# A decoder layer on one core: the key projection at the end of a step, and five other pieces at other places

## The chip, the cores and the metric

One core of a Trainium2 chip runs the whole kernel. The metric is the device time of one execution in microseconds (us), median of several runs. Engines: PE is TensorE (matmuls), DVE is VectorE, ACT is ScalarE, POOL is GpSimd, SP only issues DMAs here.

## The reference

A post-norm decoder layer for 32 sequences x of 256 tokens with 256 features, all in float32.

```python
x1 = layernorm(x + self_attention(x))      # 16 heads of 16, q and k widened to rank 32, causal softmax
x2 = layernorm(x1 + cross_attention(x1))   # 120 context rows; scores over all 256 features; mask after softmax
x3 = layernorm(x2 + ffn(x2))
# ffn: xr = mu_r*x + (1-mu_r)*x_prev, xk = mu_k*x + (1-mu_k)*x_prev   (x_prev: the token before)
#      out = sigmoid(xr @ W_r.T) * (relu(xk @ W_k.T)**2 @ W_v.T)
```

## The kernel before

One "batch" is one sequence. Work is pipelined over steps: `step(at)` handles five batches at once, each at another stage, `Batch(at, skew)` being batch `at - skew`. The stages are IN (skew 0: q and k), SCORES (2: self-attention scores and their row maxima, and v), PROBS (3: the turned scores, exp, product with V, and kx and vx for the cross-attention), CROSS (4: output projection z1, x1, cross-attention s2, g, z2) and FFN (5: x2 turned, k3, r3, v3). Steps 5 to 31 have all stages live; 0 to 4 fill the pipeline, 32 to 36 empty it.

Each engine runs its own list of operations, written out by hand in its `step`, and waits on semaphores for the others. Within a list nothing overtakes.

PE goes through six slots in the order 0, 2, 3, 1, 4, 5. In `slot(c)` it computes scores of one group of heads into `ps_s` (8 heads in slots 0 and 1, 4 in the others) and turned scores of another batch into `ps_t`. Slot after slot uses the same `ps_s` and `ps_t`, so each needs the row maximum of the slot before (DVE, L918, `max_done`) and its exp (ACT, L718, `exp_done`). Between the slots stand the projections and the rest: q (L492), z1 (L500), x2's turning (L463), k (L492), x1's turning (L463), v (L500), s2 (L649), k3 (L492), r3 (L500), g (L666), PV(0) (L594), v3 (L500), z2 (L680), PV(1) (L594), kx (L472), vx (L480). A projection in split precision is 12 matmuls: weights and data are each a high and a low part, three products are summed. For it an ACT operation writes the high part and a POOL or DVE operation the low part: xT, yT, xk, xr, k_act. q and k are split after their projection, into `parts0` and `parts1` (ACT L727, DVE L926).

All the pieces between the slots share two PSUM banks, `ps_m0` and `ps_m1`. `BANK_USERS` lists the users of each in order, with the semaphore that says a user's result has been read; `bank_free` makes PE wait for that of the user before.

DVE, in order: the maximum of slot 0; x3's statistics; the maximum of slot 2; q's low part; sum1 (L988); x1's statistics (L935, L941); the maximum of slot 3; k's low part; the mix for xk; the maximum of slot 1; the mix for xr; the maximum of slot 4; s2's maximum (L1005); s2's reciprocal (L1010) and a_nrm; the maximum of slot 5; the shift (L1021 to L1029); k_act's low part (L975); the first half of the attention output; the gated product; sum2 and x2's statistics; the second half.

The mix, on DVE, reads `dx` and `x2T` in SBUF:

```python
last = nc.vector.scalar_tensor_tensor(dst[:, k, :], dx[:, k, :], cols[:, mu, k:k + 1],
                                      x2T[:, k, 0:T], op0=ALU.mult, op1=ALU.add)
```

POOL, in order: yT's low part; x_res plus a constant; 1/deviation and offset of x3 and of x1 (L1126 to L1132); dx; xk's low part (L1156); xr's low part (L1159); x1p; xT's low part of the next batch; sum3; offset of x2.

SP issues the DMAs in order: x_in for the next batch; q's parts to DRAM; the outputs; k's parts; x_res; ctxT; the shift of this step to DRAM and back into two rows of the stack (L378, L384); and then the stack, twelve DMAs of 128 KB each (L347), which regroup q's and k's parts by head. The scores read the stack two steps after the projections, the turned scores also the shift.

Of the kernel before, what the change touches and what calls it, by code (L numbers as in the profile page):

```python
# [14 lines left out]
RING = 3  # L15
# [31 lines left out]
def decoder_layer(nc, x, x_turned, ctx_turned, mask_in, Wq, bq, WkT, bk, WvT, bv, WoT, bo, Wq_lsr_turned, Wk_lsr_turned,  # L47
# [8 lines left out]
    with es:  # L56
# [116 lines left out]
        def sems(*names):  # L173
# [9 lines left out]
        a_ = sems("xT_hi", "q_hi", "k_hi", "v_ready", "yT_hi", "x1T_ready", "a_exp_done", "g_ready",  # L183
# [12 lines left out]
                  "gated_done", "xr_ready", "xk_ready", "k_act_lo")  # L196
# [106 lines left out]
        def _(sp):  # L303
# [45 lines left out]

            def step(at):  # L350
                b = Batch(at, IN)
                if live(at + 1, IN):
                    sp.wait_ge(g_["xT_lo"], b.n + 1)
                    sp.dma_start(x_in[:], tokens(x_turned, b.n + 1).rearrange("(k p) t -> p k t", p=P)).then_inc(x_loaded, 16)
                if live(at, IN):
                    save_parts(b, 0, "q_lo")
                if live(at - 1, FFN):
# [4 lines left out]
                if live(at, IN):  # L362
                    save_parts(b, 1, "k_lo")
# [4 lines left out]
                if live(at, SCORES):  # L368
# [4 lines left out]

                    if c.n >= RING:
# [26 lines left out]
        def _(pe):  # L401
# [135 lines left out]
            def step(at):  # L537
# [84 lines left out]
                filler(4, not on[FFN] and not on[IN])  # L622
# [604 lines left out]
```

## Time and profile before

| | |
|---|---|
| median of 3 runs | 970.09 us (968.84 to 973.53) |
| the profiled execution | 973.32 us |
| its span in the profile | 971.6 us |
| PE busy | 918.1 us (94%) |
| DVE, ACT, POOL busy | 715.0, 590.1, 450.6 us |
| mean granted TensorE clock | 0.971 of full speed |

The span goes from the first instruction to the last. Busy time is that in which the engine works at something; PE's is modelled at the ends of matmuls, so it reads a little high. A duration in a timeline is that of a single operation or of several merged (x2, x8); the next operation of an engine may start before the last one's end, so what an operation costs its engine is read from start to start.

### The profile page before, as it was taken

The page shows a single profiled execution, that of the slowest core. Times are in us where ns is not written, and L with a number is a line of the kernel's source. Part 1 is how long each engine was busy: PE and PEld are TensorE (multiplying, and loading weights), DVE is VectorE, ACT ScalarE, POOL GpSimd, SP SyncE. Part 2 cuts the span into 40 slices and gives each one's busy share as a digit, 9 for nine tenths or more (in the row PEclk, how much of TensorE's full clock was granted, in tenths as well). Part 3 has the DMA queues.
Part 4 walks back from the last instruction along what each step waited for, and adds up shares of the span by engine and source line. Part 5 has one row for each costly group of instructions (what it writes and reads, how often), then busy time and mean ns, then how long its engine had stood idle before and what let it go on. Part 6 is the DMA issues. An engine that isn't in the chain of part 4 may idle for free.

```text
span 971.6 us, 25805 instructions
## 1 busy us (share of the span) xinstructions
PE 918.1 (94%) x9597; PEld 723.6 (74%) x9597; DVE 715.0 (74%) x1565; ACT 590.1 (61%) x1153; POOL 450.6 (46%) x667
## 2 busy tenths in 40 slices
PE   6789999999999999999999999999999999999975
PEld 5456778778777777777778777777778777777653
DVE  3646778788788878788778877878878887867442
ACT  2125566666776666666776666666776666656643
POOL 6202354544455455544445445454445545434453
PEclk9959999999999999999999999999999999989998
DMA  8977876656677766666688877666678777611000
GB/s 221 195 146 117 149 131 111 137 129 137 129 147 150 151 117 106 136 136 133 132 143 149 150 122 123 119 133 134 129 144 148 150 134 116 110 30 31 24 12 22
DMA packets 121447, 119.73 MB, mean 123 GB/s; under 512 B 28201, under 2 KB 104811, under 8 KB 121195
## 3 DMA queue, kind: packets, MB, share of 16 engines
q1 hardware_dynamic: 121323, 118.08, 64.3%
q8 instruction: 77, 1.26, 0.6%
q14 instruction: 47, 0.39, 0.2%
HBM read 75.05 MB, written 42.99 MB: 121 GB/s over the span
## 4 chain that ended last, share of the span: by engine, by line
PE 80%; ACT 8%; issue 5%; DVE 4%; POOL 2%; DMA 1%; SPq 0%; ACTq 0%; POOLq 0%; DVEq 0%
PE ps_m L500 20%; PE ps_m L492 11%; PE ps_o L594 9%; PE ps_s L513 8%; PE ps_t L513 5%; PE ps_s L528 4%; PE ps_m L463 4%; PE ps_m L649 3%; PE ps_m L472 3%; ACT p L718 3%; ACT sum L735 3%; PE ps_m L680 3%; PE ps_m L666 3%; PE ps_m L480 3%; PE ps_t L528 2%
## 5 line engine op out<-in xcount | busy, mean ns | idle before, releaser
L918 DVE TENSOR_REDUCE row_max<-ps_s 128x4 f32<-128x1024 f32 (+1 forms) x192 | 233.2, 1215 | 76.7 <-PE ps_s L528 76.5
L718 ACT ACTIVATE p<-ps_t 128x1024 f32<-128x1024 f32 x192 | 196.4, 1023 | 45.2 <-PE ps_t L528 45.1
L513 PE MATMUL ps_s<-stack 48*128 48x128 f32 (+1 forms) x1024 | 109.1, 313 | 15.5 <-DVE row_max L918 6.4
L827 ACT COPY kxT<-ps_m 128x240 f32<-128x240 f32 x32 | 11.5, 358 | 169.0 <-PE ps_m L472 169.0
L513 PEld LDWEIGHTS ps_s<-stack 48*128 48x128 f32 x1024 | 73.3, 190 | 53.4 <-DVE row_max L918 20.0
L1100 POOL TENSOR_TENSOR xT_lo<-x_in,xT_hi 128x512 fp32r<-128x512 f32 x32 | 41.4, 1293 | 151.4 <-ACT xT_hi L705 151.4
L594 PE MATMUL ps_o<-p,v_pad 128*32 128x256 f32 (+1 forms) x2048 | 96.3, 329 | 0.0
L513 PE MATMUL ps_t<-stack 50*128 50x128 f32 (+1 forms) x1024 | 93.1, 281 | 1.9 <-ACT p L718 1.4
L594 PEld LDWEIGHTS ps_o<-p,v_pad 128*32 128x32 f32 x2048 | 57.4, 109 | 43.2 <-issue 21.2
L1171 POOL TENSOR_TENSOR sum<-r_tanh,x 128x512 f32<-128x512 f32 x32 | 40.9, 1279 | 83.4 <-DVE r_tanh L1039 83.4
L513 PEld LDWEIGHTS ps_t<-stack 50*128 50x128 f32 x1024 | 75.3, 192 | 5.0 <-ACT p L718 2.7
L935 DVE BATCH_NORM_STATS2 bn<-sum 128x6 f32<-128x256 f32 x192 | 71.9, 417 | 3.6 <-POOL sum L1171 1.4
L1156 POOL TENSOR_TENSOR xk_lo<-r_tanh,xk_hi 128x512 fp32r<-128x512 f32 x32 | 41.3, 1290 | 66.5 <-ACT xk_hi L772 66.5
L1126 POOL TENSOR_TENSOR var<-mv,eps 128x2 f32<-128x2 f32 x96 | 18.8, 196 | 114.2 <-DVE mv L941 110.7
L1129 POOL TENSOR_TENSOR rstd<-var,neg_half 128x2 f32<-128x2 f32 x96 | 66.9, 697 | 0.0
L528 PE MATMUL ps_s<-mask_s,identb 64*64 64x256 bf16 (+1 forms) x768 | 66.1, 334 | 0.0
L528 PE MATMUL ps_t<-mask_t,identb 64*64 64x256 bf16 (+1 forms) x768 | 61.8, 312 | 0.0
L1159 POOL TENSOR_TENSOR xr_lo<-dx,xr_hi 128x512 fp32r<-128x512 f32 x32 | 41.3, 1290 | 40.9 <-ACT xr_hi L788 40.9
L1140 POOL TENSOR_TENSOR yT_lo<-y32T,yT_hi 128x512 fp32r<-128x512 f32 x32 | 40.6, 1270 | 40.9 <-ACT yT_hi L743 40.9
L952 DVE STREAM_TRANSPOSE yu<-ps_o 128x512 f32<-128x512 f32 x64 | 44.8, 701 | 16.6 <-PE ps_o L594 16.6
L968 DVE SCALAR_TENSOR_TENSOR dx<-dx,cols,x2T 128x256 f32<-128x256 f32 x64 | 54.0, 882 | 0.0
L926 DVE SCALAR_TENSOR_TENSOR parts<-ps_m,cols,parts 128x256 fp32r<-128x256 f32 x64 | 28.0, 480 | 29.8 <-ACT parts L727 29.8
(167 smaller groups left out, 2715.0 us busy)
## 6 DMA issues: line engine op xcount, KB each, us to landing
stack<-parts_dram SPq DMA_DIRECT2D x384, 128.0 KB, 5.8
parts_dram<-parts SPq DMA_DIRECT2D x64, 512.0 KB, 4.8
x_in<-in_x_turned SPq DMA_DIRECT2D x32, 256.0 KB, 8.2
x_res<-in_x SPq DMA_DIRECT2D x32, 256.0 KB, 4.0
out_x<-sum SPq DMA_DIRECT2D x64, 128.0 KB, 4.7
ctxT<-in_ctx_turned SPq DMA_DIRECT2D x32, 120.0 KB, 3.7
shift_dram<-shift_turned SPq DMA_DIRECT2D x64, 16.0 KB
stack<-shift_dram SPq DMA_DIRECT2D x64, 16.0 KB
```

Of the source, the lines that this page charges most:

```text
L492: last = nc.tensor.matmul(bank[:, a * T:(a + 1) * T], ww, ss, start=(e == 0), stop=(e == len(terms) - 1))
L500: last = nc.tensor.matmul(bank[:, j * C:(j + 1) * C], ss, ww, start=(e == 0), stop=(e == len(terms) - 1))
L513: nc.tensor.matmul(target[:, at_h:at_h + width], left[b.slot][r0:r0 + rows_n, h // 2, rows_at:rows_at + P], right[b.slot][r0:r0 + rows_n, ...
L528: last = nc.tensor.matmul(o, identb[r, 64 * half:64 * half + 64], mask[r, block, 0:o.shape[1], :], start=False, stop=True, skip_group_chec ...
L594: last = nc.tensor.matmul(ps_o[VW * j:VW * (j + 1), half, at_g + T - width:at_g + T], v_pad[b.slot][:, tile, h, :], p[c][:, at_h:at_h + wi ...
L718: nc.scalar.activation(p[c][:], ps_t[:], ACT.Exp).then_inc(exp_done[c], 1)
L918: nc.vector.tensor_reduce(row_max[:, :, j0:j0 + nj, tile], ps_s[:].rearrange("p (g j w) -> p g j w", j=nj, g=2), AX_X, ALU.max) \
L935: last = nc.vector.bn_stats(bn[i][:, j, :], src[:, j, :])
L952: nc.vector.transpose(turned, ps_o[:, half, :]).then_inc(yu_turned[half], 1)
L968: last = nc.vector.scalar_tensor_tensor(dst[:, k, :], dx[:, k, :], cols[:, mu, k:k + 1], x2T[:, k, 0:T], op0=ALU.mult, op1=ALU.add)
L1100: g.tensor_tensor(xT[b.slot][1][:], x_in[:], xT[b.slot][0][:].bitcast(F32), ALU.subtract) \
L1129: g.tensor_tensor(rstd[i][:], var[i][:], neg_half[:], ALU.pow).then_inc(rstd_done[i], 1)
```

## The change

On PE, `project("k", ...)` goes to the end of the step. v goes to k's place (ahead of slot(1)), kx and PV(0) stand between slot(1) and x1's turning, vx behind s2, and k3 behind slot(5). k is split at the start of the next step, on ACT and DVE; SP saves k's parts first in the next step, and loads the stack there too, now ahead of the shift. (Step 0 keeps its own order.) x1T's copy from PSUM moves from ACT to DVE, between the two mixes. DVE takes the maximum of slot 3 ahead of x1's statistics, the maximum of slot 1 ahead of the mix for xk, and the maximum of slot 5 ahead of s2's reciprocal. ACT gets exp(3), the v copy, kx, exp(4), vx and exp(5) at places to fit; the bank lists change with the order. POOL's list stays.

```diff
         BANK_USERS = [
-            [("q", IN, v_["q_lo"]), ("x2T", FFN, a_["x2T_ready"]),
-             ("x1T", CROSS, a_["x1T_ready"]), ("s2", CROSS, a_["a_exp_done"]), ("r3", FFN, a_["r_tanh_done"]),
-             ("z2", CROSS, v_["sum2_done"]), ("vx", PROBS, a_["vx_ready"])],
-            [("z1", CROSS, v_["sum1_done"]), ("k", IN, v_["k_lo"]),
-             ("v", SCORES, a_["v_ready"]), ("k3", FFN, a_["k_relu_done"]), ("g", CROSS, a_["g_ready"]),
-             ("v3", FFN, v_["gated_done"]), ("kx", PROBS, a_["kxT_ready"])],
+            [("q", IN, v_["q_lo"]), ("x2T", FFN, a_["x2T_ready"]), ("kx", PROBS, a_["kxT_ready"]),
+             ("s2", CROSS, a_["a_exp_done"]), ("k3", FFN, a_["k_relu_done"]), ("g", CROSS, a_["g_ready"]),
+             ("z2", CROSS, v_["sum2_done"])],
+            [("z1", CROSS, v_["sum1_done"]), ("v", SCORES, a_["v_ready"]), ("x1T", CROSS, v_["x1T_ready"]),
+             ("vx", PROBS, a_["vx_ready"]), ("r3", FFN, a_["r_tanh_done"]), ("v3", FFN, v_["gated_done"]),
+             ("k", IN, v_["k_lo"])],
         ]
...
# SP
+            def stacks(b):
+
+                if b.n >= RING:
+                    before_it = Batch(b.n - RING, IN)
+                    sp.wait_ge(t_filled, before_it.chunks_done(T_ORDER, T_ORDER[-1]))
+                load_stack(b, 0, (0, 0, 1))
+                if b.n < RING:
+                    sp.wait_ge(ones_ready[b.n], 2)
+                load_stack(b, 1, (0, 1, 0))
+
             def step(at):
                 b = Batch(at, IN)
+                if live(at - 1, IN) and at > 1:
+                    save_parts(Batch(at - 1, IN), 1, "k_lo")
...
+                if at == 0:
+                    save_parts(b, 1, "k_lo")
+                    stacks(b)
...
-                if live(at, IN):
-                    save_parts(b, 1, "k_lo")
...
+                if live(at - 1, IN) and at > 1:
+                    stacks(Batch(at - 1, IN))
...
# PE
-                project("k", "Wk")
-                filler(4, scores_over and on[PROBS])
-                filler(12, cross_last)
-                filler(14, ffn_last)
-                slot(1)
-                if on[CROSS]:
-                    bank = bank_free(pe, "x1T", at)
-                    pe.wait_ge(a_["x1_ready"], X.n + 1)
-                    turn_tiles(bank, x1).then_inc(filled["f_x1T"], 1)
                 if on[SCORES]:
                     bank = bank_free(pe, "v", at)
...
+                filler(12, cross_last)
+                filler(14, ffn_last)
+                slot(1)
+                if on[PROBS]:
+                    bank = bank_free(pe, "kx", at)
+                    pe.wait_ge(ctx_loaded[Pb.n % 2], (Pb.n // 2 + 1) * 16)
+                    rows_out(bank, wx_fold, ctxT[Pb.n % 2]).then_inc(filled["f_kx"], 1)
+                PV(0)
+                if on[CROSS]:
+                    bank = bank_free(pe, "x1T", at)
+                    pe.wait_ge(a_["x1_ready"], X.n + 1)
+                    turn_tiles(bank, x1).then_inc(filled["f_x1T"], 1)
+                filler(4, first_scores)
                 slot(4)
...
+                if on[PROBS]:
+                    bank = bank_free(pe, "vx", at)
+                    tokens_out(bank, ctxT[Pb.n % 2], wT["Wxv"], tiles=1, rows=M).then_inc(filled["f_vx"], 1)
+                filler(4, first_scores)
+                slot(5)
                 if on[FFN]:
                     bank = bank_free(pe, "k3", at)
                     pe.wait_ge(g_["xk_lo"], F.n + 1)
                     rows_out_split(bank, "Wkf", xk).then_inc(filled["f_k3"], 1)
-                slot(5)
...
-                PV(0)
...
                 PV(1)
...
+                project("k", "Wk")
...
# DVE
                 row_maxima(0)
+                k_bias = [cols[:, BK, a:a + 1] for a in range(KC)]
+                if live(at - 1, IN) and at > 1:
+                    split_lo(Batch(at - 1, IN), 1, "k_hi", "k_lo", k_bias, "k")
...
+                row_maxima(3)
                 if on[CROSS]:
                     stats(0, X, sum1, v_["sum1_done"])
-                row_maxima(3)
-                if on[IN]:
-                    split_lo(A, 1, "k_hi", "k_lo", [cols[:, BK, a:a + 1] for a in range(KC)], "k")
+                row_maxima(1)
                 if on[FFN]:
                     dve.wait_ge(g_["dx_done"], F.n + 1)
                     mix(xk_f32, MUK, "xk_ready")
-                row_maxima(1)
+                if on[CROSS]:
+                    dve.wait_ge(filled["f_x1T"], X.n + 1)
+                    wait(dve, filled["f_s2"], X.n)
+                    wait(dve, v_["k_act_lo"], F.n)
+                    nc.vector.tensor_copy(flat(x1T), bank_of("x1T")[:]).then_inc(v_["x1T_ready"], 1)
                 if on[FFN]:
                     mix(xr_f32, MUR, "xr_ready")
                 row_maxima(4)
...
+                row_maxima(5)
                 if on[CROSS]:
                     dve.wait_ge(a_["a_exp_done"], X.n + 1)
...
-                row_maxima(5)
```

ACT's list of a full step becomes: yT's high part; k's high part (of the batch before); exp(0); x2; q's high part; exp(2); x3; exp(3); x2T; the v copy; x1; exp(1); kx; xk's high part; exp(4); xr's high part; vx; s2's negated maximum and a_exp; exp(5); k_act: relu, square, high part; r's tanh; g; xT's high part.

## Rows read from the trace of the kernel before

**Rows 1.** Stretch, length; busy PE, PEld, DVE, ACT, POOL; PEclk, DMA share, GB/s
```profile
488.50:515.70 27.20, 26.87 (x297) 21.55 (x296) 21.93 (x49) 18.27 (x36) 13.47 (x20) 1.00 0.75 135
842.70:900.00 57.30, 52.34 (x547) 40.95 (x546) 40.12 (x89) 33.23 (x62) 24.51 (x38) 0.91 0.25 45
```

**Rows 2.** Timeline of PE in a middle step: start, length, line, what
```profile
488.51 0.66 PE L513 MATMUL ps_s<-stack 48*128 48x128 f32 x8
...
490.11 0.39 PE L492 MATMUL ps_m<-xT_hi,hi_Wq 128*128 128x256 f32 x1
...
495.79 0.36 PE L492 MATMUL ps_m<-xT_hi,hi_Wk 128*128 128x256 f32 x1
...
497.60 0.66 PE L513 MATMUL ps_s<-stack 48*128 48x128 f32 x8
...
499.46 0.63 PE L463 MATMUL ps_m<-ident,sum 128*128 128x128 f32 x4 [0.20 <-ACT sum L735]
...
499.84 0.36 PE L500 MATMUL ps_m<-hi_Wv,xT_hi 128*128 128x256 f32 x1
...
502.45 1.15 PE L649 MATMUL ps_m<-kxT,x1T 128*128 128x120 f32 x8
...
503.37 0.36 PE L492 MATMUL ps_m<-xk_hi,hi_Wkf 128*128 128x256 f32 x1
...
504.94 0.50 PE L513 MATMUL ps_s<-stack 48*128 48x256 f32 x4
...
505.95 0.39 PE L500 MATMUL ps_m<-hi_Wr,xr_hi 128*128 128x256 f32 x1
...
508.43 1.51 PE L594 MATMUL ps_o<-p,v_pad 128*32 128x256 f32 x32
...
509.86 0.39 PE L500 MATMUL ps_m<-hi_Wvf,k_act_hi 128*128 128x256 f32 x1
...
513.79 1.15 PE L472 MATMUL ps_m<-ctxT,wx_fold 128*128 128x120 f32 x8
...
515.74 0.44 PE L513 MATMUL ps_s<-stack 48*128 48x128 f32 x4
```

**Rows 3.** Timeline of DVE in the same step; then one tile (min/median/max), one group
```profile
495.40 0.75 DVE L935 BATCH_NORM_STATS2 bn<-sum 128x6 f32<-128x256 f32 x2
...
496.35 1.19 DVE L918 TENSOR_REDUCE row_max<-ps_s 128x4 f32<-128x1024 f32 x1
...
501.09 1.40 DVE L968 SCALAR_TENSOR_TENSOR dx<-dx,cols,x2T 128x256 f32<-128x256 f32 x1
...
502.81 1.21 DVE L918 TENSOR_REDUCE row_max<-ps_s 128x4 f32<-128x1024 f32 x1
...
503.94 0.39 DVE L1005 TENSOR_REDUCE s_max<-ps_m 128x2 f32<-128x240 f32 x1
...
505.43 0.17 DVE L1010 RECIPROCAL s_rec<-s_sum 128x2 f32<-128x2 f32 x1 [1.09 <-ACT a_exp L796]
...
508.80 0.69 DVE L975 TENSOR_TENSOR k_act_lo<-x1T,k_act_hi 128x512 fp32r<-128x512 f32 x1 [0.53 <-ACT k_act_hi L816]
...
L968 DVE SCALAR_TENSOR_TENSOR dx<-dx,cols,x2T x64: 471/480/1503, 119.6 to 953.9; 128x256 f32<-128x256 f32 x64
...
L863 DVE COPY wx_fold<-ps_t 128x512 f32<-128x512 f32 x1 | 0.7, 684 | 0.0
```

**Rows 4.** Timeline of POOL in the same step
```profile
497.65 0.19 POOL L1132 TENSOR_TENSOR offset<-neg_mean,rstd 128x2 f32<-128x2 f32 x1
...
500.93 1.28 POOL L1156 TENSOR_TENSOR xk_lo<-r_tanh,xk_hi 128x512 fp32r<-128x512 f32 x1 [2.08 <-ACT xk_hi L772]
```

**Rows 5.** Timeline of ACT in the same step
```profile
498.23 1.08 ACT L735 ACTIVATE sum<-sum,offset,rstd 128x256 f32<-128x256 f32 x2
...
500.24 0.61 ACT L772 CAST xk_hi<-r_tanh 128x512 fp32r<-128x512 f32 x1
```

**Rows 6.** The chain that ended last, where a shift is on it
```profile
79.12 1.91 DMA shift_dram<-shift_turned
```

More of the change, by code:

```diff
@@ L621, in step @@
                 slot(3)
-                filler(4, not on[FFN] and not on[IN])
+                filler(4, not on[FFN] and not on[SCORES])
                 if on[FFN]:
@@ L661, in step @@
                     tokens_out_split(bank, xr, "Wr").then_inc(filled["f_r3"], 1)
+                filler(4, not on[FFN] and not on[CROSS])
                 if on[CROSS]:
@@ L761, in step @@
                         .then_inc(a_["x2T_ready"], 1)
-                exp(3)
-                if on[IN]:
-                    split_hi(A, 1, "k_hi", [cols[:, BK, a:a + 1] for a in range(KC)], "k")
-                if on[CROSS]:
-                    wait(act, filled["f_x1T"], X.n)
-                    normalise(0, X, x1, sum1, "x1_ready")
-                exp(1)
-                if on[FFN]:
-                    act.wait_ge(v_["xk_ready"], F.n + 1)
-                    wait(act, filled["f_k3"], F.n)
-                    nc.scalar.copy(xk[0][:], xk_f32).then_inc(a_["xk_hi"], 1)
-                if on[CROSS]:
-                    act.wait_ge(filled["f_x1T"], X.n + 1)
-                    wait(act, filled["f_s2"], X.n)
-                    wait(act, v_["k_act_lo"], F.n)
-                    nc.scalar.copy(flat(x1T), bank_of("x1T")[:]).then_inc(a_["x1T_ready"], 1)
                 if on[SCORES]:
@@ L784, in step @@
                     last.then_inc(a_["v_ready"], 1)
+                if on[CROSS]:
+                    wait(act, filled["f_x1T"], X.n)
+                    normalise(0, X, x1, sum1, "x1_ready")
+                exp(1)
+                if on[PROBS]:
+                    act.wait_ge(filled["f_kx"], Pb.n + 1)
+                    wait(act, filled["f_s2"], Pb.n - 2)
+                    nc.scalar.copy(flat(kxT[Pb.slot]), bank_of("kx")[:, 0:KC * M]).then_inc(a_["kxT_ready"], 1)
+                if on[FFN]:
+                    act.wait_ge(v_["xk_ready"], F.n + 1)
+                    wait(act, filled["f_k3"], F.n)
+                    nc.scalar.copy(xk[0][:], xk_f32).then_inc(a_["xk_hi"], 1)
+                exp(4)
                 if on[FFN]:
@@ L788, in step @@
                     nc.scalar.copy(flat(xr[0]), flat(xr_f32)).then_inc(a_["xr_hi"], 1)
-                exp(4)
+                if on[PROBS]:
+                    act.wait_ge(filled["f_vx"], Pb.n + 1)
+                    wait(act, filled["f_z2"], Pb.n - 2)
+                    nc.scalar.copy(vx[Pb.slot][:], bank_of("vx")[0:M, 0:C]).then_inc(a_["vx_ready"], 1)
                 if on[CROSS]:
@@ L798, in step @@
                     last.then_inc(a_["a_exp_done"], 1)
+                exp(5)
                 if on[FFN]:
@@ L806, in step @@
                         .then_inc(a_["k_act_ready"], 1)
-                exp(5)
+                if on[FFN]:
+                    act.wait_ge(a_["k_act_ready"], F.n + 1)
+                    wait(act, filled["f_v3"], F.n)
+                    nc.scalar.copy(flat(k_act[0]), flat(k_act_f32)).then_inc(a_["k_act_hi"], 1)
                 if on[FFN]:
@@ L812, in step @@
                         .then_inc(a_["r_tanh_done"], 1)
-                if on[FFN]:
-                    act.wait_ge(a_["k_act_ready"], F.n + 1)
-                    wait(act, filled["f_v3"], F.n)
-                    nc.scalar.copy(flat(k_act[0]), flat(k_act_f32)).then_inc(a_["k_act_hi"], 1)
                 if on[CROSS]:
@@ L977, in step @@
                 row_maxima(0)
+                k_bias = [cols[:, BK, a:a + 1] for a in range(KC)]
+                if live(at - 1, IN) and at > 1:
+                    split_lo(Batch(at - 1, IN), 1, "k_hi", "k_lo", k_bias, "k")
                 if live(at - 1, FFN):
```

47 lines of the change are left out of this document (16 added, 31 removed).

## The prediction

> **What bounds the kernel now.** I read the busy time by stretch first. In one middle step the matrix engine is busy for 26.87 of 27.20 us at the full clock, 2.4 GHz, while DVE has 21.93, ACT 18.27 and POOL 13.47 [rows 1]. So TensorE (PE) sets the step, and what can be won there is only its waiting. Next came the timeline of PE. From one first slot to the next it takes 27.23 us (488.51 to 515.74) [rows 2]. Two waits are in it. The key projection takes 1.81 us to the start of slot(1), where the same twelve matmuls of v, less the slot behind them, take 502.45 - 499.84 - 1.01 = 1.60: 0.21 us are a wait, and it is for the row maximum that ends at 496.35 + 1.19 = 497.54 [rows 2, 3]. From slot(1) to x1's turning there are 1.86 us, where slot(0), which is the same work, takes 490.11 - 488.51 = 1.60: 0.26 us, for ACT's x1, whose two operations end at 499.31 [rows 2, 5]. Without waits the step is 27.23 - 0.47 = 26.76 us. That is all the steady steps can give back: 27 steps with everything live times 0.47 is 12.7 us.
>
> **What moves on PE.** No matmul of a full step is added or removed, so 26.76 us stays the floor. With t = 0 at slot(0), everything up to x2's turning stays (7.28 us to what follows it). Then v (1.60) to 8.88, slot(1) (1.60) to 10.48, kx (half of the 1.95 of kx and vx) to 11.46, PV(0) (1.43) to 12.89, x1's turning (0.40) to 13.3, slot(4) (1.01) to 14.3, s2 (0.92) to 15.2, vx to 16.2, slot(5) to 17.2, k3 (1.57), r3 and g (2.48 together), v3 [rows 2]. The wait for the maximum of slot 3 goes: that maximum now runs ahead of x1's statistics. The wait for x1 goes too: v, kx and PV(0) lie ahead of the turning, and x1 is ready near 11.8, against 12.9.
>
> **What is late next: three waits.**
> First, slot(5). x1T's copy goes from ACT to DVE, behind the turning, and the mix for xr and the maximum of slot 4 stand behind it in DVE's order. The turning starts at 12.89 and is full 0.65 later (its row has 0.63). Before does not show this copy on DVE; the nearest row, a copy of 512 elements from PSUM, took 684 ns [rows 3], and ACT's work of that size 0.61 [rows 5]. I take 0.68 of these two bounds, since it is the same engine and memory. So the xr mix can start near 14.2. The mix reads two SBUF tensors. In before its first half took 1.40 us where the median of the 64 is 0.48: it started at 501.09 with POOL in xk_lo from 500.93 to 502.21, and ended 0.28 after POOL; the next maximum started 0.60 after POOL's end [rows 3, 4]. Does POOL hold it again? x1's statistics start near 8.2 (slot 3 is full at 6.9, the maximum ahead of them takes 1.13). From their start to the offset's end there were 497.84 - 495.40 = 2.44 us, so x1 starts at 10.64; xk_hi follows x1 by 2.01 plus some 0.3 for kx's copy, which now lies between, takes 0.61, and xk_lo starts at 13.6 and ends at 14.9 [rows 3 to 5]. It is again ahead of the mix. So the maximum of slot 4 starts at 15.5 and not at 15.0, and ends 1.21 later at 16.7; PE follows 0.06 behind. Slot(5) starts at 16.8 where it could at 16.2: **0.6 us** (0.07 if POOL is out of the way).
> The Trainium skill, "SBUF — State Buffer", section "Who interferes with whom", says that a DVE instruction with two SBUF inputs and a GpSimd instruction that reads SBUF exclude each other, and that the second to issue waits until the first is finished. The 1.40 us row agrees, and it speaks against this order of work; a reading without that rule would have 0.07 in place of 0.6.
> Second, k3. It now uses the bank that s2 used, right behind slot(5), and its wait is for the softmax of s2 (before, this bank wait fell to r3, a whole k3 later). s2's maximum starts 1.13 after slot 4's, and the sums are in 1.49 after that (503.94 to 505.43) [rows 3]: 15.5 + 2.62 = 18.1, and PE 0.1 later. Slot(5) ends at 17.8. **0.45 us**, and this one stays in every case in which slot(5) waits for slot 4's maximum, since both hang on the same start. Queued behind k3 on PE is the rest of the step.
> Third, v3. Slot(5) and PV(0) used to lie between k3 and v3 (503.37 to 509.86, 6.49 us) [rows 2]; now only r3 and g do: 1.57 + 2.48 = 4.05 us. k_act takes k3's 1.57 and 0.1, three operations of ACT at 0.61 with 0.03 between, 1.92, and DVE's 0.69, then 0.1 to PE [rows 3, 5]: 4.4 us. **0.37 us.**
> Sum of a full step: 26.76 + 0.6 + 0.45 + 0.37 = 28.2 us, 0.95 over 27.23.
> A further one is a toss-up. DVE's y operation of the first half, with two SBUF inputs, now starts as soon as k_act_lo is done, within 0.1 us of POOL's xT_lo. If POOL is first, y loses 1.2 us (the 1.28 of such an operation), yT_hi is at 1.5 in the next step instead of 0.5, ACT runs behind, and slot(2)'s probabilities wait some 0.3 us for exp(0). Ends 0 and 0.3; I take the middle, 0.15.
>
> **What costs nothing, and its cover.** Splitting k at the start of the next step adds 0.8 us to ACT and DVE ahead of the maximum of slot 2; that one still ends at 5.6, ahead of slot(3) at 5.9, and z1's bank, which now needs k's split, is wanted at 4.2 with the split done at 3.5. Covers are 0.2 us and 0.7. The v copy, kx and vx on ACT lie in its idle time. On SP's queue k's save goes ahead of x_in, and the twelve stack loads, 1.57 MB, ahead of the shifts instead of behind them. At 135 GB/s [rows 1] they take 11.6 us, are issued from about 9.6 (behind x_res and ctxT) and drain near 22 to 24. The shift, ready at 20, then queues behind them. With an idle queue its first transfer took 1.91 us [rows 6]; the second is issued when the first is in, and I count it the same, so it lands at 26 to 27.5. Slot(0)'s probabilities want it at 28.8 (27.4 without my three waits). Hidden, by 1.3 us or more; without that cover each us late is a us in every step.
>
> **Ends of the run.** Start: batch 1's stacks are loaded in step 2 instead of at its beginning, and PE has an idle stretch there to hide part of their 11.6 us; bounds 0 and half of it, 6, and I take +2, as the weights hold PE in that place too. Steps 32 and 33 took 57.3 us at a mean clock of 0.91: the clock was at its lower level, 1.2 GHz, for 0.09 x 57.3 / 0.5 = 10 us, which cost 5, after PE had idled where the projections are missing [rows 1]. Now v stands where k was missing, and some of that idling goes: ends -5 and 0, I take -3. In step 34 kx and PV(0) fill PE's wait for x1: ends -3 and +1, I take -1.
>
> **Sum.** 27 x (0.95 + 0.15) = +29.7; with +2, -3 and -1 it is +27.7. The profiled span of 971.6 becomes 999. Outside the span lie 1.7 us (973.32 - 971.6), and the median of the runs is 3.2 below the profiled one, so the median goes from 970.1 to 998.
>
> **Rivals.**
> 1. The mix escapes POOL (0.07 instead of 0.6), if xk_lo is done by 14.2. Then 0.07 + 0.45 + 0.37 - 0.47 = +0.42 a step, 27 x 0.42 - 2 = +9: 979. For it: the margin is only 0.7 us of a chain with six links. Against: both ends of that chain hang on the same step.
> 2. The clock gives way. In steps 32 and 33 idling of that kind was followed by the lower level [rows 1], and two of my new waits, 0.6 and 0.45, lie within 2 us. If it falls in a third of the steps, each time for a third of those 10 us, a fall costs half of 3.3 us: 9 x 1.7 = +15: 1013. Against: in the full steps before, with 0.47 us of waits, it was at 1.00.
> 3. On the other side, faster: the waits that go are all there is. It needs the chain from the turning through slot 4's maximum to be 0.7 us shorter than I make it (the copy and both halves of the mix ahead of slot(4)'s end). Then slot(5) and k3 wait for nothing, the third wait of 0.37 at most stays, and the ends decide: 27 x (0.37 - 0.47) - 2 = -5: 965. It decides when that maximum starts before 14.5.
> 4. Old and new waits balance: slot(5) and v3 don't wait, k3 waits its 0.45. Then 27 x (0.45 - 0.47) - 2 = -2.5: 968, within 5 us of before. It takes a quicker copy and an unblocked mix, as rival 3, but less of both.
> 5. The shift is late: each us costs 27. With my waits it has room, so it would come only on top of case 1 or 3; I give it 0.03 (1000 or more).
>
> **Chances.** My forecast 0.50, rival 1 0.17, rival 2 0.13, rival 3 0.08, rival 4 0.09, rival 5 0.03. A measurement of this kernel tells about 0.5%, 5 us, from no change. Faster 0.08; same 0.11 with rival 1's lower edge; slower 0.81. The range goes from rival 1 to rival 2 with their widths: 976 to 1018. The forecast's own range is 989 to 1006.
>
> **What the changed profile would show.** In a middle step: PE's period 28.2 instead of 27.2; PE busy near 26.9 of it; waits ahead of slot(5) for DVE's row maximum, ahead of k3 for ACT's a_exp, and ahead of v3 for k_act_lo; none ahead of slot(1) and x1's turning; the xr mix still with one operation over 1 us and POOL's xk_lo beside it; the clock at 1.00. Wrong would be: a period under 27.2, the mix at 0.48 twice, PE waiting for the shift's landing at slot(0), or a clock under 1.00 in the middle.

## The result, and the profile after

The changed kernel takes 1009.5 us (median of four runs, 1008.2 to 1013.6), the kernel before beside it on the same chip 969.5 (963.8 to 973.5): 1.0425 times as long, with an interval of 1.037 to 1.048. The forecast was 998, the range 976 to 1018. The profiled execution took 1009.6 us with a span of 1007.9, 36.3 over the span of before.

Where the 36.3 us lie can be read from three starts of q on PE. The q of step 5, the first full step, starts at 114.71 (before 108.66): +6.05. From there to the q of step 31 it takes 732.31 us (before 708.40): +23.91, which is 0.92 for each of 26 steps. From that q to the end it takes 160.88 us (before 154.54): +6.34.

First the windows of the kernel after, columns as in [rows 1]: a middle step, steps 3 and 4, two short stretches in step 4, and the end.

```profile
507.34:535.50 28.16, 27.24 (x298) 21.62 (x297) 22.28 (x50) 17.72 (x35) 13.51 (x21) 1.00 0.66 129
54.00:85.00 31.00, 22.77 (x254) 16.45 (x256) 12.98 (x21) 10.12 (x16) 3.77 (x3) 0.89 0.62 117
85.00:113.00 28.00, 25.49 (x240) 18.80 (x232) 17.79 (x38) 11.11 (x22) 4.95 (x10) 0.82 0.64 121
...
104.00:106.00 2.00, 1.09 (x4) 0.65 (x4) 1.86 (x7) 0.53 (x2) 0.00 (x0) 0.90 0.93 122
106.00:108.00 2.00, 1.96 (x4) 1.18 (x4) 0.58 (x2) 0.45 (x1) 1.26 (x1) 0.50 0.14 21
...
930.00:1007.90 77.90, 55.87 (x389) 41.48 (x385) 32.42 (x89) 32.12 (x61) 32.98 (x55) 0.86 0.05 18
```

The middle step has 27.24 us of PE's work in 28.16, at the full clock, so PE waits some 0.9 us in each step. All full steps are at that clock (113.11 to 842.00: 1.00). Step 4 and the end are at 0.82 and 0.86. For the same two places of the kernel before, the windows are these (step 3, step 4, the end):

```profile
54.00:83.00 29.00, 28.21 (x236) 19.53 (x232) 13.19 (x21) 9.65 (x16) 1.28 (x1) 0.67 0.61 109
83.00:107.00 24.00, 21.83 (x248) 16.45 (x248) 16.04 (x35) 12.76 (x24) 6.85 (x11) 1.00 0.81 147
...
900.00:971.60 71.60, 54.48 (x382) 37.65 (x381) 25.48 (x79) 32.90 (x64) 31.22 (x50) 0.90 0.06 19
```

Now PE's timeline in the same middle step of the kernel after; it answers to [rows 2]. A bracket at the end of a row is an idle time and what ended it.

```profile
507.34 0.66 PE L522 MATMUL ps_s<-stack 48*128 48x128 f32 x8
...
510.54 0.51 PE L522 MATMUL ps_s<-stack 48*128 48x256 f32 x4
...
511.72 0.38 PE L509 MATMUL ps_m<-hi_Wo,yT_hi 128*128 128x256 f32 x1
...
514.77 0.36 PE L509 MATMUL ps_m<-hi_Wv,xT_hi 128*128 128x256 f32 x1
...
516.38 0.66 PE L522 MATMUL ps_s<-stack 48*128 48x128 f32 x8
...
520.49 0.66 PE L472 MATMUL ps_m<-ident,sum 128*128 128x128 f32 x4
521.08 0.50 PE L522 MATMUL ps_s<-stack 48*128 48x256 f32 x4
...
523.08 1.03 PE L489 MATMUL ps_m<-T_Wxv,ctxT 128*120 128x256 f32 x4
524.03 0.50 PE L522 MATMUL ps_s<-stack 48*128 48x256 f32 x4
...
525.50 0.38 PE L501 MATMUL ps_m<-xk_hi,hi_Wkf 128*128 128x256 f32 x1 [0.39 <-ACT a_exp L811]
...
529.99 0.36 PE L509 MATMUL ps_m<-hi_Wvf,k_act_hi 128*128 128x256 f32 x1 [0.54 <-DVE k_act_lo L984]
...
535.50 0.66 PE L522 MATMUL ps_s<-stack 48*128 48x128 f32 x8
```

Between the starts of z1 and slot(1) stand the same pieces as in before, and v takes 1.61 us to slot(1), so the wait at slot(1) is gone; so is that at x1's turning. Slot(5) comes 0.95 us after vx, as long as vx takes: no wait. Two waits are marked, at k3 (from start to start 0.46 us over slot(5)'s 1.01) and at v3 (0.60). A third has no mark: slot(2) takes 1.18 us to z1, where slots of that size take 1.01 elsewhere. The last 0.17 us are where pieces meet: from x1's turning to the slot behind it 0.59 us, where v behind the turning came after 0.38 [rows 2].

The DVE operations behind the turning, and that on y, of the kernel after ([rows 3] of before):

```profile
521.18 0.69 DVE L1015 COPY x1T<-ps_m 128x512 f32<-128x512 f32 x1 [1.29 <-PE ps_m L472]
521.79 1.06 DVE L977 SCALAR_TENSOR_TENSOR dx<-dx,cols,x2T 128x256 f32<-128x256 f32 x2
522.77 1.21 DVE L927 TENSOR_REDUCE row_max<-ps_s 128x4 f32<-128x1024 f32 x1
523.90 0.39 DVE L1022 TENSOR_REDUCE s_max<-ps_m 128x2 f32<-128x240 f32 x1
...
529.15 0.69 DVE L984 TENSOR_TENSOR k_act_lo<-x1T,k_act_hi 128x512 fp32r<-128x512 f32 x1 [1.68 <-ACT k_act_hi L828]
...
530.79 1.34 DVE L967 TENSOR_TENSOR y<-yu,o_rec 128x256 f32<-128x256 f32 x1
```

POOL in the same step ([rows 4] of before):

```profile
520.89 1.28 POOL L1173 TENSOR_TENSOR xk_lo<-r_tanh,xk_hi 128x512 fp32r<-128x512 f32 x1 [1.94 <-ACT xk_hi L795]
...
530.56 1.29 POOL L1117 TENSOR_TENSOR xT_lo<-x_in,xT_hi 128x512 fp32r<-128x512 f32 x1 [4.23 <-ACT xT_hi L714]
```

And ACT ahead of k3 ([rows 5] show it elsewhere in the step):

```profile
524.14 0.37 ACT L804 COPY vx<-ps_m 120x256 f32<-120x256 f32 x1 [0.40 <-PE ps_m L489]
524.41 0.21 ACT L807 ACTIVATE s_neg<-s_max 128x2 f32<-128x2 f32 x1
524.65 0.36 ACT L811 ACTIVATE a_exp<-ps_m,s_neg 128x120 f32<-128x120 f32 x1
```

### The profile page after: what moved, and what is told of

Read it like the earlier page. It is cut to its first block, busy times and chain, and to the rows that moved or that the text cites. A ratio compares the mean times of both kernels' runs of the same rounds, so it can differ in the third digit from the quotient of the medians.

```text
span 1007.9 us, 25790 instructions
## 1 busy us (share of the span) xinstructions
PE 926.9 (92%) x9585; PEld 728.1 (72%) x9593; DVE 726.2 (72%) x1597; ACT 572.4 (57%) x1121; POOL 451.4 (45%) x667
## 4 chain that ended last, share of the span: by engine, by line
PE 74%; ACT 10%; issue 5%; DVE 5%; DMA 3%; SPq 1%; POOL 1%; ACTq 0%; POOLq 0%; DVEq 0%
PE ps_m L509 15%; PE ps_m L501 15%; PE ps_o L603 8%; PE ps_s L522 8%; PE ps_t L522 6%; PE ps_s L537 4%; PE ps_m L472 4%; PE ps_m L481 3%; PE ps_m L661 3%; PE ps_m L489 3%; PE ps_m L695 3%; PE ps_t L537 2%; ACT x1T L823 2%; DVE k_act_lo L984 2%; ACT k_act_hi L828 2%
## 5 line engine op out<-in xcount | busy, mean ns | idle before, releaser
L752 ACT CAST yT_hi<-y32T 128x512 fp32r<-128x512 f32 x32 | 19.8, 619 | 199.3 <-issue 195.2
L522 PE MATMUL ps_s<-stack 48*128 48x128 f32 (+1 forms) x1024 | 108.7, 312 | 14.8 <-DMA stack<-parts_dram 10.5
L984 DVE TENSOR_TENSOR k_act_lo<-x1T,k_act_hi 128x512 fp32r<-128x512 f32 x32 | 22.2, 693 | 59.9 <-ACT k_act_hi L828 59.9
L501 PE MATMUL ps_m<-xk_hi,hi_Wkf 128*128 128x256 f32 x128 | 40.1, 314 | 16.0 <-ACT a_exp L811 13.9
L509 PE MATMUL ps_m<-hi_Wvf,k_act_hi 128*128 128x256 f32 x128 | 38.6, 302 | 16.0 <-DVE k_act_lo L984 16.0
```

The costliest lines, as they stand in the source:

```text
L501: last = nc.tensor.matmul(bank[:, a * T:(a + 1) * T], ww, ss, start=(e == 0), stop=(e == len(terms) - 1))
L509: last = nc.tensor.matmul(bank[:, j * C:(j + 1) * C], ss, ww, start=(e == 0), stop=(e == len(terms) - 1))
L522: nc.tensor.matmul(target[:, at_h:at_h + width], left[b.slot][r0:r0 + rows_n, h // 2, rows_at:rows_at + P], right[b.slot][r0:r0 + rows_n, ...
L984: nc.vector.tensor_tensor(t[1][:], value[:], t[0][:].bitcast(F32), ALU.subtract).then_inc(v_[lo], 1)
```

## The experiments

Twelve kernels, all built on the changed kernel but the last two. "Ratio" is to the kernel before, run beside each.

### Whose chain holds k3

```diff
# e1_mix_first, DVE
+                if on[FFN]:
+                    mix(xr_f32, MUR, "xr_ready")
                 if on[CROSS]:
                     dve.wait_ge(filled["f_x1T"], X.n + 1)
...
-                if on[FFN]:
-                    mix(xr_f32, MUR, "xr_ready")
                 row_maxima(4)
```

> The changed kernel with one thing moved: on DVE the mix for xr goes ahead of x1T's copy. Theory: k3's wait of 0.46 us hangs on DVE's chain copy, mix, slot 4's maximum, s2's maximum, exp of s2. The mix then runs at about 12.5 us of the step, ahead of POOL's xk_lo at 13.6 (both halves near 0.48 us, none at 1 us), slot 4's maximum starts at 14.8 and not 15.4, and the sums of s2 are in at 17.5, before slot(5) ends at 17.7. The step shrinks from 28.16 to 27.7 us: 27 x 0.46 = 12 us less than the changed kernel, near 997. Rival (k3 waits for its bank whatever DVE does, since s2's softmax is that long): under 3 us less. Rival (the time saved is lost again at v3): v3's wait grows by what k3's loses.

Measured: ratio 1.041 (1.034 to 1.048), period 28.15 as before the edit, and the same 0.39 us mark at k3. DVE did what the edit wants: the mix took 0.87 us for its two halves, and s2's maximum ended 0.72 us ahead of s_neg (523.43 + 0.41 to 524.56), where in the changed kernel it ends 0.12 ahead. But ACT, in the rows of this kernel, still came late to s_neg:

```profile
524.29 0.37 ACT L804 COPY vx<-ps_m 120x256 f32<-120x256 f32 x1 [0.40 <-PE ps_m L489]
524.56 0.21 ACT L807 ACTIVATE s_neg<-s_max 128x2 f32<-128x2 f32 x1
```

ACT's list has vx's copy ahead of s_neg (the negated maximum of s2), and PE ends vx only just ahead of slot(5). So my theory of one chain over DVE fell, and a new one took its place: two chains of nearly equal length end at a_exp, one over DVE's mix, one over ACT's order.

```diff
# e5_vx_late: the edit above, and on ACT
-                if on[PROBS]:
-                    act.wait_ge(filled["f_vx"], Pb.n + 1)
-                    wait(act, filled["f_z2"], Pb.n - 2)
-                    nc.scalar.copy(vx[Pb.slot][:], ...
                 if on[CROSS]:
                     act.wait_ge(v_["s2_max_done"], X.n + 1)
...
                     last.then_inc(a_["a_exp_done"], 1)
+                if on[PROBS]:
+                    act.wait_ge(filled["f_vx"], Pb.n + 1)
+                    wait(act, filled["f_z2"], Pb.n - 2)
+                    nc.scalar.copy(vx[Pb.slot][:], ...
```

> The changed kernel with the xr mix ahead of x1T's copy, as in the run before, and in addition vx's copy behind a_exp on ACT. The run with the mix alone showed s2's maximum done at 523.84 and ACT waiting until 524.29 for PE's vx, which stands ahead of s2's negated maximum. Theory: k3's wait was held by two chains of the same length, DVE's and ACT's order; with both shortened it goes, and the step takes 27.7 us, 12 us less than the changed kernel. Rival: it is neither, and the step stays at 28.15. If exp(5) is later by the vx copy, it costs nothing, since k_act waits for k3.

Measured: ratio 1.026 (1.019 to 1.032), period 27.68, no wait at k3; that at v3 stays (0.54 by its mark). With both chains cut the step wins 0.47 us, with DVE's alone nothing. ACT's alone was not run. By the rows of the changed kernel it would win at most 0.12 us: s2's maximum ends there at 524.29, and s_neg, which starts at 524.41, can't start ahead of that.

```diff
# e2_banks
+            [("q", ...), ("x2T", ...), ("kx", ...), ("s2", ...), ("r3", ...), ("v3", ...)],
+            [("z1", ...), ("v", ...), ("x1T", ...), ("vx", ...), ("k3", ...), ("g", ...), ("z2", ...), ("k", ...)],
```

> The changed kernel with other PSUM banks only: k3, g, z2 and k in the second bank, r3 and v3 in the first, so that k3 follows vx and not s2. The order of all work stays. Theory: k3's wait of 0.46 us is for s2's reader of the bank, nothing else; it goes, v3's wait stays at 0.60, and the step takes 27.7 us: 12 us less, near 997. Rival (k3 waits for xk_lo or for the pipeline of PE): no change. A new wait is possible at k, whose bank is now freed by sum2, at 26.5 us of the step; if it costs 0.2 us, the gain is 7 us.

Measured: ratio 1.023 (1.015 to 1.031), period 27.70. The wait at k3 is gone although a_exp is as late as ever (k3 starts at 520.49, a_exp's last operation ends at 520.89), and v3's stays. So k3 waited for nothing but its bank.

### v3, and PV(0) as cover

```diff
# e3_pv0_back, PE
-                PV(0)
                 if on[CROSS]:
                     bank = bank_free(pe, "x1T", at)
...
                 filler(7, ffn_last)
+                PV(0)
```

> The changed kernel with PV(0) back behind g, as in the kernel before: between k3 and v3 there is again 1.44 us more. Theory: v3's wait of 0.60 us goes. x1's turning comes 1.4 us earlier, at 11.7, and x1 is ready at 11.8: a wait of 0.2 us there. Slot(5) comes at 15.2 with slot 4's maximum not done before 16, as the mix still lies between: a wait of 0.7 to 1.0 us, and k3's 0.46 stays. Together the step is 28.4 to 28.7 us and the kernel 5 to 15 us slower than the changed one. Rival (v3's wait is all that PV(0)'s place costs): the step is 27.6, 15 us faster.

Measured: ratio 1.042 (1.034 to 1.049), period 28.37. PE's marked waits in one full step of this kernel:

```profile
516.70 0.63 PE L472 MATMUL ps_m<-ident,sum 128*128 128x128 f32 x4 [0.16 <-ACT sum L744]
...
521.05 0.50 PE L522 MATMUL ps_s<-stack 48*128 48x256 f32 x4 [0.74 <-DVE row_max L927]
522.42 0.38 PE L501 MATMUL ps_m<-xk_hi,hi_Wkf 128*128 128x256 f32 x1 [0.30 <-ACT a_exp L811]
```

The wait at v3 is gone, as it should be with 1.43 us more between k3 and v3. What replaces it is the very wait I had forecast at slot(5), at 0.74 us, and x1's turning waits again. PV(0) pays 0.6 at one place and is missed for more at another. The whole run was to be 5 to 15 us slower and took the same time (median 1009.4): the full steps cost 5.7 us more, but the q of step 5 starts at 108.91, 5.8 us earlier. Of these, 4.5 us lie ahead of the q of step 3, where the edit changes nothing; how far such starts differ from trace to trace is told below.

### y and POOL

```diff
# e6_xlo_late, POOL
-                if at > 0:
-                    x_lo(at + 1)
                 if on[FFN]:
                     pool.wait_ge(v_["gated_done"], F.n + 1)
...
                     g.tensor_tensor(sum3[:], gated[:], x2[:], ALU.add)...
+                if at > 0:
+                    x_lo(at + 1)
```

> The changed kernel with POOL's xT_lo behind sum3, nothing else. Theory: DVE's first y operation took 1.34 us instead of 0.43 because POOL had started xT_lo 0.2 us earlier; without it DVE's tail is 0.9 us earlier, yT_hi comes at 0.4 us of the next step and not at 1.3, exp(0) is done in time, and slot(2)'s turned scores do not wait: 0.1 to 0.2 us a step, 3 to 5 us, near 1005. Rival (slot(2) is longer for another reason): y falls to 0.43 us and the step stays at 28.16.

Measured: ratio 1.035 (1.029 to 1.041), period 28.00, 0.16 less. y took 0.42 us in place of 1.34, and slot(2) no longer waits (1.02 us to z1). The changed kernel's rows above show the conflict in its pure form: POOL's xT_lo starts 0.23 us ahead of y and ends at 531.85; y, which takes 0.42 alone, ends at 532.13. The Trainium skill, "SBUF — State Buffer", section "Who interferes with whom", says that a DVE instruction with two SBUF inputs, as y is, and a GpSimd instruction that reads SBUF, as xT_lo is, exclude each other, and that the second waits until the first is finished. The rows agree: y ends only after xT_lo.

### All at once

```diff
# e7_combined: the edits of e2_banks, e3_pv0_back, e1_mix_first and e6_xlo_late together
```

> The changed kernel with four things together: the other banks, PV(0) back behind g, the xr mix ahead of x1T's copy, and xT_lo behind sum3. Theory: the waits at k3 and v3 go, slot(5)'s does not come since slot 4's maximum starts as soon as the slot is full, slot(2)'s goes, and some 0.15 us at x1's turning stay: 26.95 + 0.15 = 27.1 us a step, 0.1 less than the kernel before. With the ends of the run as in the run with PV(0) back, near 972, the same as the kernel before within 0.7%. Rival (the key projection at the end of the step costs something by itself, through the late stacks and shifts): PE waits for a landing at slot(0), and the step stays over 27.5.

Measured: ratio 1.021 (1.015 to 1.027), period 27.67, 0.57 over what I expected. The waits at k3, v3, slot(5) and slot(2) are gone, and one has come at s2. DVE of this kernel shows why; PE was through with the turning (start 510.56, 0.63 long) by 511.19, and s2 started at 512.67, where slot(4)'s end would have let it start near 512.2:

```profile
511.09 0.87 DVE L976 SCALAR_TENSOR_TENSOR dx<-dx,cols,x2T 128x256 f32<-128x256 f32 x2
511.88 0.68 DVE L1016 COPY x1T<-ps_m 128x512 f32<-128x512 f32 x1
```

With the mix ahead of the copy, and PV(0) no longer in front of the turning, the copy waits for the mix and s2 for the copy. x1's turning waits too, 0.15 us by its mark.

### The start of the run

The new order loads the stacks of step 1 only in step 2. In the trace of after, PE waits for them ahead of step 3's slot(0):

```profile
57.28 1.12 PE L522 MATMUL ps_s<-stack 48*128 48x128 f32 x8 [6.54 <-DMA stack<-parts_dram]
```

```diff
# e4_stacks_early
-                if live(at - 1, IN) and at > 1:    (SP, ACT and DVE)
+                if live(at - 1, IN) and at > 2:
...
-                if at == 0:
+                if at <= 1:
```

> The changed kernel, but batch 1's k is split and its stack loaded in step 1 as in the kernel before (the rule that held for step 0 holds for steps 0 and 1). Full steps are not touched. Theory: step 3 began at 57.3 us instead of 52.6 because PE waited for that stack; it begins at 52.6 again, and step 5 begins at 108 to 109 instead of 113.2: 4 to 5 us less, near 1005. Rival (the ramp's loss is the clock at its lower level in steps 3 and 4, whatever the stack does): the start of step 5 moves by less than 1.5 us.

Measured: ratio 1.037 (1.030 to 1.043). The q of step 3 starts 3.6 us earlier (55.31), but the q of step 5 only 0.4 (114.28): step 3 then lasted 31.14 us in place of 26.54. The rival held in this trace. What was won there the clock took back in the next step (0.68 in 54 to 85), as in the kernel before, where step 3 lasts 30.29 us at 0.67. It doesn't do so each time: e10_k3_ramp below, with the same edit to the stacks, starts step 3 at 55.37 and needs 26.88 us for it, at 0.92 in 54 to 82. The whole run was still 4.9 us shorter, in its last steps (156.16 us from the q of step 31). The edit changes nothing there, and the next kernel, whose edit is in step 4 alone, has the same gain at the same place (156.18). So it can't be put down to either edit. What these traces do show there is the clock: 0.94 from that q to the end in both, 0.90 in the trace of the changed kernel.

In step 4 of the changed kernel, PE idles 1.90 us ahead of g and 0.61 ahead of z2, and from 106 the clock is at 0.50, 1.2 GHz, as the window above shows; it is 0.76 in 111 to 114.

```profile
104.34 1.09 PE L682 MATMUL ps_m<-T_Wp,a_nrm 128*120 128x256 f32 x4 [1.90 <-DVE a_nrm L1032]
...
106.04 2.05 PE L695 MATMUL ps_m<-g_sb,vx 120*128 120x256 f32 x4 [0.61 <-ACT g_sb L838]
```

The next kernel fills these idle times (the expectation has 1.6 and 0.9 us for them, where the rows have 1.90 and 0.61):

```diff
# e8_fill_step4, PE
+                if X.n == 0:
+                    pe.wait_ge(yu_turned[1], Pb.n)
+                    keep_clock(ps_o[:, 1, :], 8)       # 8 matmuls that nothing reads
                 if on[CROSS]:
                     bank = bank_free(pe, "g", at)
...
+                if X.n == 0:
+                    keep_clock(ps_o[:, 1, :], 8)
                 if on[CROSS]:
                     bank = bank_free(pe, "z2", at)
```

> The changed kernel with 16 matmuls that nobody reads in step 4 alone, 8 ahead of g and 8 ahead of z2, where PE idled for 1.6 and 0.9 us and the granted clock then fell to 0.5 from 106 to 112 us. Theory: half of the 6 us that step 5 begins late is the clock: it stays at 1.00 through z2, PV(1) and k, and step 4 takes 26.5 to 27 us instead of 29.3. Full steps stay at 28.16. 2 to 3 us less. Rival (step 4 is long by its waits alone): the same length, or longer by the matmuls, up to 2 us.

Measured: ratio 1.039 (1.033 to 1.045); step 4 lasts 26.88 us in place of 29.27, as forecast. The q of step 5 starts only 1.4 us earlier (113.32), since step 3, ahead of the edit, took 28.02 us in place of 26.54. The span is 6.2 us shorter, and 4.7 of them are those of the last steps. The windows of this kernel over the same stretch:

```profile
104.00:106.00 2.00, 1.94 (x10) 1.02 (x9) 1.90 (x8) 0.40 (x1) 0.00 (x0) 1.00 1.19 154
106.00:108.00 2.00, 2.00 (x11) 1.12 (x10) 1.22 (x4) 0.98 (x2) 0.76 (x1) 1.00 0.39 49
```

### Back to the cover: k3 ahead of slot(5)

The first runs say that each wait came where a piece of work that had hidden a chain was taken away. The plain cure is not to shorten chains but to put the cover back:

```diff
# e9_k3_first, PE (and POOL's xT_lo as in e6_xlo_late)
+                    rows_out_split(bank, "Wkf", xk).then_inc(filled["f_k3"], 1)
                 filler(4, first_scores)
                 slot(5)
...
+                    tokens_out(bank, ctxT[Pb.n % 2], wT["Wxv"], tiles=1, rows=M).then_inc(filled["f_vx"], 1)
...
-                    rows_out_split(bank, "Wkf", xk).then_inc(filled["f_k3"], 1)
# banks
+            [("q", ...), ("x2T", ...), ("kx", ...), ("s2", ...), ("vx", ...), ("g", ...), ("z2", ...)],
+            [("z1", ...), ("v", ...), ("x1T", ...), ("k3", ...), ("r3", ...), ("v3", ...), ("k", ...)],
```

ACT copies vx behind k_act's high part, and DVE takes the maximum of slot 5 behind a_nrm again.

> The changed kernel with k3 put back ahead of slot(5) and vx behind it (s2 and vx in the first bank, k3 and r3 in the second; ACT copies vx behind k_act's high part; the maximum of slot 5 behind a_nrm again), and POOL's xT_lo behind sum3. Theory (each wait of the change is a piece of work that lost its cover): slot(5) lies again between k3 and v3 (1.0 us more than the 0.60 that v3 waited), k3's bank is free since x1T's copy, y no longer meets POOL. Expected: no wait at k3 or v3, period 28.15 - 0.46 - 0.60 - 0.16 = 26.95 us, full steps about 5 to 7 us shorter than in the kernel before, the start and the end of the run still some 11 us longer: 975 us. Rival (what takes the place of the waits is again an equally long chain): vx now waits for a_exp, or r3 for k_act's relu, 0.3 us or more, period 27.3 or more, 985 us.

Measured: 973.4 us, ratio 1.0021 (0.9987 to 1.0054): level with the kernel before. The period is 27.18 us. Of the 0.97 us won, 0.46 are k3's, 0.16 y's and 0.35 v3's, which still waits 0.25. What that wait is for stands in DVE's rows of this kernel:

```profile
511.10 1.21 DVE L927 TENSOR_REDUCE row_max<-ps_s 128x4 f32<-128x1024 f32 x1
...
512.96 0.65 DVE L984 TENSOR_TENSOR k_act_lo<-x1T,k_act_hi 128x512 fp32r<-128x512 f32 x1
```

k_act's high part was done at 511.73 (ACT, 511.11 and 0.62 long), but the maximum of slot 5 and the three operations of the shift stood ahead of its low part. Start and end together cost 3.5 us over before: the q of step 5 starts at 113.07 (+4.4), and from the last q to the end it is 153.6 (-0.9).

```diff
# e10_k3_ramp: e9_k3_first with e4_stacks_early and e8_fill_step4
```

> The kernel of the run with k3 ahead of slot(5), and with both edits at the start of the run: the stacks of step 1 loaded in step 1, and sixteen unread matmuls in step 4. Theory: the two gains add to it, 4.9 and 3.8 us in the runs that had them alone: 975 - 8 = 967 us, the time of the kernel before. Rival: both act on the same thing, the clock in steps 4 and 5, and add up to less than 5 us: 970 us or more.

Measured: 973.8 us, ratio 1.0025 (0.9993 to 1.0057). The profiled execution starts step 5 at 109.99, 3.1 us earlier, and its span is 4.1 shorter (969.4), yet the medians of ten runs each are the same. The executions of one kernel differ by up to 10 us here (967.7 to 977.2), so a single trace doesn't prove such a gain. The theory missed. It had added up gains of 4.9 and 3.8 us, and in the traces of both kernels 4.7 us of the gain lie in the last steps, where neither edit acts.

### The kernel before without its own two waits

```diff
# e11_v_first: before, with v ahead of x1's turning (PE), and v's copy ahead of x1T's (ACT)
```

> The kernel before with one piece moved: v ahead of x1's turning, on PE and on ACT; all else stays. Theory: the 0.26 us that PE waited there for x1 have v's 1.6 us as cover, x1T's copy is then 0.1 us from holding s2: period 27.23 - 0.26 + 0.0 to 0.1, 5 us over the run: 965 us. Rival: s2 takes over the wait (slot(4) alone covers x1T's copy on ACT), period 27.2, no change.

```diff
# e12_v_max3: the same, and on DVE
+                row_maxima(3)
                 if on[CROSS]:
                     stats(0, X, sum1, v_["sum1_done"])
-                row_maxima(3)
```

Besides, exp(1) goes ahead of x1 on ACT, and dx ahead of x1's deviation on POOL.

> The same, and the maximum of slot 3 ahead of x1's statistics on DVE, exp(1) ahead of x1 on ACT, and dx ahead of x1's deviation on POOL. Theory: both waits of the kernel before (0.21 and 0.26 us) go; x1 comes 1.2 us later and just makes its turning (margin about 0): period 26.8 to 26.95, 8 to 12 us over the run: 960 us. Rival: x1 comes too late by 0.2 us or more, or the chain through xk delays k3: period 27.0 or more, 965 us or more.

Measured: ratios 1.0054 (1.0023 to 1.0085) and 1.0119 (1.0074 to 1.0164); both were to be faster. The periods are 27.16 and 27.61. In the second, slot(1)'s wait is gone (1.60 us from k to it). PE's marked waits of the second:

```profile
501.69 0.39 PE L500 MATMUL ps_m<-hi_Wv,xT_hi 128*128 128x256 f32 x1 [0.25 <-DVE parts L926]
...
503.64 0.63 PE L463 MATMUL ps_m<-ident,sum 128*128 128x128 f32 x4 [0.25 <-ACT sum L735]
```

v follows k in the same bank, and so waits for k's split; with x1's turning between them it never had. And x1 starts 1.8 us later in the step (11.52 us after slot(0), before 9.72), more than the 1.6 us of v can cover. Half of that is the maximum's, which now stands ahead of x1's statistics: x1's offset was ready at 501.45, 10.56 us after slot(0). The other half is exp(1)'s, which now stands ahead of x1 on ACT:

```profile
501.49 1.03 ACT L718 ACTIVATE p<-ps_t 128x1024 f32<-128x1024 f32 x1 [0.77 <-PE ps_t L528]
502.41 1.08 ACT L735 ACTIVATE sum<-sum,offset,rstd 128x256 f32<-128x256 f32 x2
```

So the second kernel fails by a part of its own edit too; the maximum without exp(1)'s move was not run. In the first, v's wait is 0.11 us and the step gains 0.07, some 2 us over the run. Its trace loses them again at the start, where the q of step 3 comes 3.3 us later than in before (57.50) and that of step 5 3.7 us later (112.33), and at the end (+1.7). What delays step 3 there stays open. No version here is faster than the kernel before.

## Why the prediction was right

The mechanism, the direction and the range were right, the total 11 us short (8.6 in the span: +27.7 against +36.3). That it came so near is in part luck. Over 27 full steps slot(5)'s 0.6 us, which didn't come, are 16 us too many in the sum. Against them stand 13 us that the ends took over what I gave them, 6 us at v3 and 5 us of the floor, all too few.

- **What bounds the kernel**, right: PE sets the step, its own two waits went, and new ones came in greater size. The floor of 26.76 us was 0.17 too low: I had taken the distance between two pieces as a property of the first, and it is one of the pair (below).
- **Slot(5), 0.6 us**: measured 0. This is the term that failed. The maximum of slot 4 started at 15.43 us of the step, as forecast (15.5), and 0.60 after POOL's end, as in before. But the hold by POOL was small: the chain started 0.3 later, so the xr mix met xk_lo near its end and was held for 0.19 us (0.98 from start to start, where an unheld pair in e1_mix_first took 0.79), against 0.53 in my sum. Its first half took 0.66 us; the sign that I had named, one operation over 1 us, didn't come. What I had not carried over is that PE itself comes later: by slot(2)'s 0.17 and the meetings of pieces ahead of it, 0.5 in all. It reached slot(5) at 16.69, when the maximum was just in, where I had it at 16.2. A wait late in a list is reckoned against all the waits ahead of it. e3_pv0_back has it, at 0.74, with PE 1.43 us earlier.
- **k3, 0.45**: measured 0.46. But my sentence that it stays in every case in which slot(5) waits, "since both hang on the same start", names one cause where there are two, and ties it to a wait that didn't come. ACT's copy of vx holds it nearly as long (e1_mix_first, e5_vx_late).
- **v3, 0.37**: measured 0.60. k3 takes 1.51 us, r3 and g behind it 2.38, 3.89 in all in place of 4.05, and the chain 4.49 in place of 4.4.
- **The toss-up at y, 0.15**: measured 0.16 to 0.17 (e6_xlo_late takes it away). POOL came first, the case for which I had 0.3; y lost 0.92 us by it and not 1.2. The middle of two ends fitted, and no more.
- Sum of a step: 26.76 + 0.17 + 0.46 + 0.60 + 0.17 = 28.16 us, against 27.23 + 1.10 = 28.33 forecast. Over 26 steps +28.6 us were forecast and +23.9 came.
- **The shift and the stacks**, right in the full steps: no wait of PE for a DMA is marked in them.
- **The start**, wrong in size. I took +2 and it was +6.05, at the upper bound of 6. The q of step 3 comes 4.66 later, behind the wait for the stacks, of which e4_stacks_early takes back 3.6; then step 3 was 3.75 us shorter and step 4 5.14 longer. By the windows step 4 had 0.18 x 28 / 0.5 = 10.1 us at the lower level, which cost up to 5 us, and e8_fill_step4 won 2.4 us of its length back. The size of the start is that of one pair of traces: in seven other kernels here whose steps 0 to 2 are those of the changed kernel, the q of step 3 starts at 57.15 to 58.98, and in an eighth (e3_pv0_back) at 54.41.
- **The end**, wrong. The rest of step 31 takes 1.1 us more, as any full step. For steps 32 and 33 I took -3, since idle times would be filled. They take 56.8 us (before 57.25), -0.4: the clock there was 0.94 and 0.88, a mean of 0.91 as before [rows 1], so nothing was given back. For step 34 I took -1, and it was +0.6. Steps 35 and 36, which I had at nothing without a reason, took 5.1 us more. The rows below show what stands in them: in step 35 PE waits 4.38 us for z1's input (before 2.43), and 2.31 for k3's bank, which is a wait of the new order.

```profile
928.41 0.36 PE L500 MATMUL ps_m<-hi_Wo,yT_hi 128*128 128x256 f32 x1 [2.43 <-POOL yT_lo L1140]
...
961.54 0.36 PE L509 MATMUL ps_m<-hi_Wo,yT_hi 128*128 128x256 f32 x1 [4.38 <-POOL yT_lo L1157]
...
973.22 0.58 PE L501 MATMUL ps_m<-xk_hi,hi_Wkf 128*128 128x256 f32 x1 [2.31 <-ACT a_exp L811]
```

(The first row is of before, the others of after.) The clock has a share as well. By the windows of 0.86 and 0.90 the last stretch has 0.14 x 77.9 / 0.5 = 21.8 us at the lower level, before 0.10 x 71.6 / 0.5 = 14.3; half of the difference is 3.7 us. That is arithmetic on two windows. How the end divides between these waits and the clock stays open, for e4_stacks_early and e8_fill_step4 have waits of 4.37 and 2.30 us at the same two places and take 4.7 us less than the changed kernel from the q of step 31 on. Of the +6.34 us only the other 1.6 are in all three traces.

Rival 1 (979) had slot(5) right, but not by its own cause: xk_lo ended at 14.8 us of the step, not by 14.2. It took v3 at its low size and the ends at -2. Rival 2's fall of the clock in full steps didn't come: 1.00 throughout, with 1.2 us of waits in a step.

## What to carry to other kernels

A piece of work between producer and user is cover: before moving it, list every chain that runs beneath it, the ACT and DVE orders included, and give each its length. Where two chains of equal length end at one wait, cutting one shows nothing, and neither is cleared by it. Count the cover in the order of the step, since a wait upstream pays for one downstream. And before you credit an edit with a gain, see whether the gain lies where the edit acts.

## What the runs showed of the hardware

- **Distances belong to pairs.** From x1's turning to the next piece it takes 0.38 us when that is v [rows 2], and 0.59 when it is slot(4) (0.53 to 0.59 in the nine other kernels with this order that I read, without a wait marked there). I have no explanation that a run singles out.
- **The clock.** In step 4 it went to 1.2 GHz after idle times of 1.90 and 0.61 us, 1.1 us apart; with both filled it stayed at 1.00. The same idle time doesn't always end alike. In e4_stacks_early the fall came within g, behind 1.89 us and ahead of the second idle time (0.75 in 104 to 105, 0.50 in 105 to 106). In e3_pv0_back 1.90 us ahead of g were followed by no fall (1.00 in 100 to 109); there PV(0) stands between g and z2. In the kernel before, 1.11 us ahead of a slot in step 33 (873.81 to 874.92) were followed by 0.66 in 875 to 880, and 1.14 us ahead of g in step 4 by 1.00. In the full steps the waits of 0.46 and 0.60 us left it at 1.00. At the start of the run the low stretches lie at other places from kernel to kernel: steps 3 and 4 are at 0.67 and 1.00 in before, at 0.89 and 0.82 after.
- **DVE beside POOL.** An operation of 0.42 us took 1.34 when POOL had started 0.23 us ahead of it, and ended 0.28 us after POOL (y and xT_lo in the changed kernel). The first half of the xr mix, 0.48 us alone, ended 0.28 us after POOL's xk_lo in both kernels, and took 1.40 us in the one before and 0.66 in the changed one.
